# Dense attention: turning the probabilities by 32 by 32 squares and DMAs instead of on TensorE

## What is computed

```python
def _sparse_attention(x, src, dst, wq, bq, wk, bk, wv, bv, wo, bo):
    q = (x @ wq + bq).reshape(N, H, Dh) * Dh ** (-0.5)
    k = (x @ wk + bk).reshape(N, H, Dh)
    v = (x @ wv + bv).reshape(N, H, Dh)
    scores = jnp.einsum('ehd,ehd->eh', q[src], k[dst])
    smax = jax.ops.segment_max(scores, src, num_segments=N)
    ex = jnp.exp(scores - smax[src])
    denom = jax.ops.segment_sum(ex, src, num_segments=N)
    attn = ex / denom[src]
    out = jax.ops.segment_sum(attn[:, :, None] * v[dst], src, num_segments=N)
    return out.reshape(N, D) @ wo + bo

for i in range(4):
    y = _cond_layer_norm(x, cond, s1_w[i], s1_b[i], b1_w[i], b1_b[i])
    x = x + _sparse_attention(y, ...)
    y = _cond_layer_norm(x, cond, s2_w[i], s2_b[i], b2_w[i], b2_b[i])
    x = x + relu(y @ m_w1[i] + m_b1[i]) @ m_w2[i] + m_b2[i]
```

## Time and profile before

| | |
|---|---|
| median of 3 runs | 2674.96 us (2674.15 to 2680.72) |
| the profiled execution's own time | 2671.21 us |
| its span, first to last instruction | 2669.5 us |
| PE / DVE / ACT / POOL busy, share of the span | 97% / 52% / 32% / 15% |
| DMA traffic | 154.71 MB, mean 58 GB/s |

### The profile page before, as it was taken

The page is one execution under the profiler, slowest core; times in us unless marked ns, Lnnn a source line. Parts: engine busy times, 40 slices in busy tenths (PEclk is TensorE's granted clock), DMA queues, the critical chain, the costliest instruction groups (busy, mean ns, idle before and its releaser), DMA issues. The chain is left out here.

```text
span 2669.5 us, 29597 instructions
## 1 busy us (share of the span) xinstructions
PE 2578.7 (97%) x10736; PEld 1534.9 (57%) x10736; DVE 1396.1 (52%) x3067; ACT 850.7 (32%) x1775; POOL 397.7 (15%) x396
## 2 busy tenths in 40 slices
PE   8999899999999999999999999999999998999994
PEld 4665545456776555777555677655577754533341
DVE  7986741515665532666551566653266654523344
ACT  5875532212442120444111244312044412302221
POOL 2004120102000200200200200020020012515551
PEclk9999999999999999999999999999999999999997
DMA  6301011420000110000010000011000001569636
GB/s 172 121 21 48 1 43 45 114 67 24 1 1 1 41 36 23 18 1 1 22 39 32 24 1 1 1 41 36 18 22 1 1 17 55 189 198 328 215 89 212
DMA packets 84372, 154.71 MB, mean 58 GB/s; under 512 B 31909, under 2 KB 32389, under 8 KB 81887
## 3 DMA queue, kind: packets, MB, share of 16 engines
q1 hardware_dynamic: 60702, 106.12, 12.8%
q0 software_dynamic: 20784, 41.80, 4.8%
q10 hardware_dynamic: 2741, 4.89, 0.7%
HBM read 207.61 MB, written 27.34 MB: 88 GB/s over the span
## 5 line engine op out<-in xcount | busy, mean ns | idle before, releaser
L1942 ACT ACTIVATE g_prob<-g_prob,g_row_max 125x1250 f32<-125x1250 f32 x160 | 214.0, 1338 | 710.6 <-DVE g_row_max L1876 710.6
L1682 PE MATMUL psum<-cols,w 128*128 128x500 f32 (+1 forms) x1120 | 393.2, 510 | 1.2 <-PEq L88 1.2
L1744 PE MATMUL psum<-g_k_cols,g_q_cols 128*125 128x512 f32 (+1 forms) x960 | 362.9, 513 | 1.9 <-DVE g_row_max L1873 1.9
L1758 PE MATMUL psum<-cols,rows 125*128 125x250 f32 x1600 | 364.0, 374 | 0.1
L1758 PEld LDWEIGHTS psum<-cols,rows 125*128 125x128 f32 x1600 | 302.7, 189 | 34.6 <-issue 3.8
L1682 PEld LDWEIGHTS psum<-cols,w 128*128 128x128 f32 x1120 | 209.9, 189 | 173.1 <-issue 165.0
L1873 DVE CUSTOM_DVE_ANT_0 g_prob<-psum,ln_count 125x1250 f32<-125x1250 f32 x160 | 233.5, 1459 | 75.2 <-PE psum L1744 75.2
L1744 PEld LDWEIGHTS psum<-g_k_cols,g_q_cols 128*125 128x125 f32 x960 | 168.0, 187 | 161.8 <-issue 159.1
L1883 DVE COPY cols<-psum 125x500 f32<-125x500 f32 x160 | 108.6, 679 | 199.2 <-PE psum L1773 199.2
L1773 PEld LDWEIGHTS psum<-ident,g_prob 125*125 125x125 f32 x1600 | 199.4, 188 | 9.0 <-issue 1.9
L1996 POOL TENSOR_TENSOR xbuf<-xbuf,g_bias_rows 125x512 f32<-125x512 f32 x40 | 63.2, 1618 | 937.0 <-DVE rows L1617 937.0
(11 more groups left out here) (346 smaller groups left out, 3446.7 us busy)
## 6 DMA issues: line engine op xcount, KB each, us to landing
m_eb<-in_L_ffn_expert_b SPq DMA_DIRECT2D x54, 192.0 KB, 5.8
w<-in_L_gnn_m_w SPq DMA_DIRECT2D x8, 1024.0 KB
slot_rows<-p_kf SPq DMA_DIRECT2D x1, 7128.0 KB, 33.5
rows<-slot_rows SPq DMA_DIRECT2D x54, 132.0 KB, 3.4
m_ew<-in_L_ffn_expert_w SPq DMA_DIRECT2D x4, 1536.0 KB, 11.0
w<-in_L_mix_W SPq DMA_DIRECT2D x4, 1024.0 KB, 5.1
w<-in_L_gnn_wq SPq DMA_DIRECT2D x4, 1024.0 KB, 5.3
w<-in_L_gnn_wk SPq DMA_DIRECT2D x4, 1024.0 KB
```

Source lines behind the costliest of these rows:

```text
L1682: ins = c.pe.matmul(c.bank(group_bank(g), width), wt[:, k, o * 128:(o + 1) * 128], y_cols[:, k, start:start + width], start=(k == 0), stop ...
L1744: ins = pe.matmul(psum[0:P, start:start + width], q_cols[:, h, t * P:(t + 1) * P], k_cols[:, h, start:start + width], start=True, stop=True)
L1758: ins = pe.matmul(c.bank(6 + g % 2, 2 * P), v_rows[:, j, h * 128:(h + 1) * 128], turned_prob[:, g % 2, j, :], start=(j == 0), stop=(j == N ...
L1942: s.activation(prob[:, u, :], prob[:, u, :], ACT.Exp, bias=row_max[:, u, 1:2], accum_out=row_max[:, u, 2:3]).then_inc(exp_made, 1)
```

## The change

- The PE transposes (`turn_probs` on PE) and the copies of their results (on DVE and ACT) are gone. DVE instead turns the 128 x 1280 probabilities of a step in 32 x 32 squares in one instruction (`turn_squares`), from SBUF to a `square` buffer in SBUF. `prob` is widened to 128 x 1280 and cleared once by POOL.
- A square then still lies in the partition quarter of its queries. For each pair of steps SP issues 4 x 4 = 16 DMAs (`turn_sp`), one for each source and destination quarter, each of 32 partitions x 2560 contiguous bytes (80 KB), from `square` to `turned`, SBUF to SBUF. Each has two slots: `square` lies over w[0], w[1] and part of w[2], `turned` in the widened `cols`.
- The product with the reciprocal row sum goes from DVE to ACT (`normalise`).
- Scores alternate between banks 0 to 2 and 3 to 5, and `scores(n)` waits for the read of step n - 2 only.
- `weigh` runs five steps behind (WEIGH_LAG = 5, before 3). Keys are now in ten blocks of 128 (the last of 98), and a weighing matmul has 256 columns, in runs of 32, where it had 250 contiguous ones.
- At the end of the steps the order on PE is: rest of pair 17, outputs 0 and 1, pair 18, two norm starts, outputs 2, pair 19.
- wo has a buffer of its own, which it shares with the conditioning weights; these get their ones and zeros again in each layer. m_w1, m_w2 and the next wq are loaded only when the last DMAs of the turning have landed.

```diff
+SQUARE = 32
+KEY_BLOCKS = -(-N // 128)
+SIDE = 128 // SQUARE
+TURNED_SLOTS = 2
+TURNED_SLOT = 2 * KEY_BLOCKS * 128
...
+    WEIGH_LAG = 5
+    score_at = lambda n: n % 2 * 3 * BANK
...
+        wo = sb("g_wo", [128, KC, D])
+        cond_w = wo[0:COND_ROWS]
+        prob = sb("g_prob", [128, 2, KEY_BLOCKS * 128])
...
+        square = [w_flat[:, s * TURNED_SLOT:(s + 1) * TURNED_SLOT].rearrange("p (b u f) -> p b u f", b=SIDE, u=2)
+                  for s in range(TURNED_SLOTS)]
+        turned = [cols_mem[:, s * TURNED_SLOT:(s + 1) * TURNED_SLOT].rearrange("p (a u f) -> p a u f", a=SIDE, u=2)
+                  for s in range(TURNED_SLOTS)]
+        turned_keys = [turned[s].rearrange("p a u (j i) -> p j u a i", i=SQUARE) for s in range(TURNED_SLOTS)]
...
+        def turn_sp(l, g):
+            sp = c.sp
+            s, pair = g % 2, PAIRS * l + g
+            sp.wait_ge(squared, 2 * pair + 2)
+            if g >= 2:
+                sp.wait_ge(weighed, pair - 1)
+            for of in range(SIDE):
+                for to in range(SIDE):
+                    load(sp, turned[s][quarter(to), of], square[s][quarter(of), to]).then_inc(turned_in[s], 16)
...
+            for g in range(PAIRS):
+                if g == PAIRS // 2:
+                    sp.wait_ge(bo_added, NT * (l + 1))
+                    load_bias_row("m_b2", l)
+                turn_sp(l, g)
+            for s in range(TURNED_SLOTS):
+                sp.wait_ge(turned_in[s], 16 * SIDE * SIDE * PAIRS // 2 * (l + 1))
+            load_w(1, "m_w1", l)
+            load_w(2, "m_w2", l)
...
                 else:
-                    pe.wait_ge(score_read, STEPS * l + n)
+                    pe.wait_ge(score_read, STEPS * l + n - 1)
...
             def weigh(g, part):
                 h = 2 * g // NT
                 if part == 0:
-                    pe.wait_ge(turned_act, 2 * (STEPS * l + 2 * g + 2))
-                    pe.wait_ge(turned_dve, STEPS * l + 2 * g + 2)
+                    pe.wait_ge(turned_in[g % 2], 16 * SIDE * SIDE * ((PAIRS * l + g) // 2 + 1))
...
-            turn_probs(0)
             for n in range(2, STEPS):
                 scores(n)
-                if n >= 3:
-                    weigh((n - 3) // 2, (n - 3) % 2)
-                turn_probs(n - 1)
-            pe.wait_ge(w_in[0], 16 * (2 * l + 1))
+                if n >= WEIGH_LAG:
+                    weigh((n - WEIGH_LAG) // 2, (n - WEIGH_LAG) % 2)
+            weigh(PAIRS - 3, 1)
+            pe.wait_ge(wo_in, 16 * (l + 1))
             outputs(0)
+            outputs(1)
+            weigh(PAIRS - 2, 0)
             weigh(PAIRS - 2, 1)
-            turn_probs(STEPS - 1)
-            outputs(1)
+            norm_pe(2 * l, 0)
+            norm_pe(2 * l, 1)
+            outputs(2)
             weigh(PAIRS - 1, 0)
             weigh(PAIRS - 1, 1)
-            norm_pe(2 * l, 0)
-            norm_pe(2 * l, 1)
...
+            def turn_squares(n):
+                u, s, pair = n % 2, n // 2 % 2, PAIRS * l + n // 2
+                v.wait_ge(prob_made, STEPS * l + n + 1)
+                if n == 0:
+                    v.wait_ge(v_mm, NT * (l + 1))
+                if n % 2 == 0 and pair >= 2:
+                    v.wait_ge(turned_in[s], 16 * SIDE * SIDE * (pair // 2))
+                v.transpose(square[s][:, :, u, :].rearrange("p b (j i) -> p b j i", i=SQUARE), prob_squares[u]).then_inc(
+                    squared, 1)
...
-            turn_probs(0)
+            turn_squares(0)
+            invert_sum(1)
             for n in range(2, STEPS):
-                normalise(n - 1)
                 scores(n)
-                turn_probs(n - 1)
-            normalise(STEPS - 1)
+                turn_squares(n - 1)
+                invert_sum(n)
+            turn_squares(STEPS - 1)
...
+            for n in range(STEPS):
+                exp(n)
+                if n >= WEIGH_LAG + 1 and (n - WEIGH_LAG) % 2:
+                    take_out((n - WEIGH_LAG) // 2)
+                normalise(n)
```

More of the change, by code:

```diff
@@ L139, in build @@
             with c.stage():
[L140 removed]
+                gnn(c, x, ln_count, cond_parts, cond_w_parts, w_all, cols_mem, cols, rows, sum_dram)
         with c.stage():
@@ L1466, in performer, with gnn @@
         pool_end()
-def gnn(c, x, ln_count, cond_parts, cond_w_parts, w, y_cols, rows, sum_dram):
+def gnn(c, x, ln_count, cond_parts, cond_w_parts, w_all, cols_mem, y_cols, rows, sum_dram):
     nc, psum, ident, a = c.nc, c.psum, c.ident, c.a
+    w = [w_all[:, i] for i in range(3)]
     H = GNN_HEADS
@@ L1640, in layer_sp @@
             load_bias_row("bv", l)
[L1641 to L1646, removed]
+            if l >= 1:
+                sp.wait_ge(part_made, 3 * l)
+            load(sp, wo[:], weight_rows("L0_gnn_wo", l)).then_inc(wo_in, 16)
             sp.wait_ge(v_made, NT * (l + 1))
             load_bias_row("bo", l)
-            sp.wait_ge(bo_added, NT * (l + 1))
-            load_bias_row("m_b2", l)
+            sp.wait_ge(v_mm, NT * (l + 1))
+            for g in range(PAIRS):
[7 more added lines that the diff above has]
+            load_w(2, "m_w2", l)
             if last:
@@ L1655, in layer_sp @@
                 load(sp, v_rows, rows_view(sum_dram[:, :])).then_inc(sum_in, 16)
-                for n, done in enumerate(((o_mm, NT * L), (h_mm, 12 * L))):
-                    sp.wait_ge(*done)
+                for n in range(2):
+                    if n == 1:
+                        sp.wait_ge(h_mm, 12 * L)
                     load(sp, w[n][:].rearrange("p c o -> p (c o)")[:, 0:4 * FFN_I].rearrange("p (c o) -> p c o", c=2),
@@ L1757, in weigh @@
                 for j in range(5 * part, 5 * part + 5):
-                    ins = pe.matmul(c.bank(6 + g % 2, 2 * P), v_rows[:, j, h * 128:(h + 1) * 128],
-                                    turned_prob[:, g % 2, j, :], start=(j == 0), stop=(j == NT - 1))
+                    r = key_rows(j)
+                    ins = pe.matmul(c.bank(6 + g % 2, 256).rearrange("p (u a i) -> p u a i", u=2, a=SIDE),
+                                    rows[0:r, j, h * 128:(h + 1) * 128], turned_keys[g % 2][0:r, j],
+                                    start=(j == 0), stop=(j == KEY_BLOCKS - 1))
                 if part == 1:
                     ins.then_inc(weighed, 1)
[L1763 to L1775, removed]
             def outputs(t):
@@ L1783, in outputs @@
                 for k in range(KC):
-                    ins = pe.matmul(c.bank(t % 2, D, P), q_cols[:, k, t * P:(t + 1) * P], w[0][:, k, :],
+                    ins = pe.matmul(c.bank(t % 2, D, P), q_cols[:, k, t * P:(t + 1) * P], wo[:, k, :],
                                     start=(k == 0), stop=(k == KC - 1))
@@ L1941, in exp, with normalise @@
                 s.wait_ge(max_negated, STEPS * l + n + 1)
-                s.activation(prob[:, u, :], prob[:, u, :], ACT.Exp, bias=row_max[:, u, 1:2],
+                s.activation(prob[0:P, u, 0:N], prob[0:P, u, 0:N], ACT.Exp, bias=row_max[:, u, 1:2],
                              accum_out=row_max[:, u, 2:3]).then_inc(exp_made, 1)
+            def normalise(n):
+                u = n % 2
+                s.wait_ge(sum_step, 2 * (STEPS * l + n) + 2)
+                s.activation(prob[0:P, u, 0:N], prob[0:P, u, 0:N], ACT.Identity, scale=row_max[:, u, 3:4]).then_inc(
+                    prob_made, 1)
             def take_out(g):
@@ L1986, in layer_pool @@
             if l == 0:
-                for n, value in ((1, 0.0), (3, 0.0), (0, 1.0), (2, 1.0)):
-                    g.memset(cond_w[:, n, :], value).then_inc(ones_made, 1)
+                g.memset(prob[:], 0.0).then_inc(prob_blank, 1)
                 g.wait_ge(c.gnn_x_in, 16 * NT)
```

95 lines of the change are left out of this document (43 added, 52 removed).

## The result

The kernel after takes 2703.57 us (median of 4 runs, 2701.78 to 2705.65) beside 2674.56 for the kernel before (4 runs, 2673.25 to 2680.72): ratio 1.0108, 95% interval 1.0095 to 1.012. It is 29 us slower, where the forecast had 134 us slower.

A forecast was written before the change was run, and what follows sets the result against it. PE bound the kernel before; SP's queue would after, at 0.74 us a DMA. 18.2 + 319 x 0.74 + 3.4 + 4.34 + 4.1 = 266.1 us a layer against 232.6, +134 in all: 2809 us, range 2540 to 2870.

The forecast's parts named there:

- A step without SP: PE's time for one attention step after the change: 2.10 us of scores and 2.17 of weighing, 4.27 us together.
- The turning: DVE's turning instruction in each attention step, priced like the score pass at 1.50 us.
- Start to first issue: Start of a layer's steps: from the end of scores(0) until SP can begin its DMAs, 18.2 us.
- The gap behind pair 19: End of a layer's steps: with outputs(2) moved ahead, PE lies open waiting for the norm, 4.1 us a layer.
- the term 319 x 0.74: SP's queue over a layer's steps: from first to last of 320 DMA issues, at 0.74 us each.
- landing: End of a layer's steps: the last DMA lands 3.4 us after its issue.
- rival (B): Attention steps: no change in time, at an SP cadence of 0.635 us an issue; 2675 us, chance 0.07.
- The sign that the prediction set: Median issue of the new DMAs on SP: below 0.5 us it is (A), above 0.6 the forecast stands.
- (A): Attention steps: SP keeps up below 0.53 us an issue, PE sets the pace; -31.3 us a layer, 2550 us, chance 0.40.
- (C): DVE's turning takes 2.9 us; in (A) 28 us a layer come back, 2662 us; a tenth of (A)'s chance.
- (D): SP's queue in attention dearer, 0.79 us an issue: +49.4 us a layer, 2873 us; part of the forecast's side.
- PE's idle time also covers a spell of halved clock: Attention steps with SP as bound: PE's idle 3.3 us a pair absorbs halved-clock spells, priced at nothing.

The follow-up runs named there:

- the fillers: Unused matmuls on PE ahead of each pair's wait for its squares, added to the kernel after: 2699.40 us, ratio 1.0099.

## Why the prediction was wrong

**Right.** The bound moved to SP's queue, and the kernel got slower. A step without SP would be 4.27 us; measured 4.26. The turning: 1.50 taken, 1.506 measured. Start to first issue: 18.2 against 18.05. The bytes are hidden, as half of them showed. POOL's constants, wo, m_w1 and m_w2 cost nothing that PE's waits show. The gap behind pair 19: 4.1 forecast, 3.5 found (from the end of its matmuls, 1299.20 - 2.91 = 1296.29, to 1300.64, less the 0.86 that stood between outputs(2)'s end and outputs(3) before), and the two experiments on it show that moving outputs(2) back saves it only when PE is the bound.

**Wrong: the term 319 x 0.74.** The step that failed is "the nearest row by source and destination, by partitions and by size is the 0.74, and I take it". Measured over the layer: 0.655. That is 319 x 0.74 = 236.1 us against 208.8, 27.3 us a layer too much. The rest of the sum was off by little: landing 2.1 us (1289.6 to 1291.70) for 3.4, start -0.15, pair 19 +0.25, the gap -0.6. Together 27.3 + 1.3 + 0.15 - 0.25 + 0.6 = 29.1: 266.1 becomes 237.0, against 232.6 before, +4.4 in this layer instead of +33.5. The stretch to m_w1 has another 1.7 for outputs(3), which the sum did not have: +6.1.

The difference of two large terms, 43.6 us of transposes gone against SP's surplus, magnified an error of 13% in the cadence to a factor of over 4 in the result. That the measured time lies inside the range of 2540 to 2870 says little, since the range was made to span both ends. The kernel lies close to rival (B)'s point, 0.635; with 0.633 the sum gives 232.0, so that (B) was no thin case between two others but sat right where the third kind of row, the 64 partitions at 0.60, pointed. The sign that the prediction set, a median issue below 0.5 us for (A) and above 0.6 for the forecast, did not decide either: 0.591 lies between.

The prediction had the decisive doubt in writing, under (A): that 0.70 "may belong to 18 rows, a number that does not spread evenly". It argued it away with "all 24 SBUF to SBUF issues cost the same", but all 24 had 18 rows, and so could not tell the two explanations apart. The run with 18 rows did, at 2808 us. Its being within 1 us of 2809 is partly luck: the cadence of 0.74 is confirmed, but its four layers are 152 us longer than before the change, where the forecast had 134, and its expert stage is 13 us shorter. Why 18 rows cost the queue more stayed open.

**Rivals.** (A)'s total was right for the kernel with twelve DMAs, 2550 against 2551.37, in part by luck: -26.1 us a layer for its -31.3, and the expert stage made up most of the rest. Its condition for 16, a cadence below 0.53, was false. The estimate of 0.43 us an issue from 512 sequencer cycles that stood beside it ("DMA: Bandwidth & Descriptors" in the Trainium skill) is too low here: 0.59 on SP, 0.61 on ACT; and its word that the time to initiate a DMA is usually small beside the DMA does not carry over to many small ones from one queue, as four DMAs fewer a pair made 134 us in the layers. (C) is out at 1.506. (D), 0.79, is out.

**A price of 0 that was wrong in another way.** "PE's idle time also covers a spell of halved clock" holds inside the steps, as the fillers showed. It does not hold behind the last wait of a layer, where outputs(3) took 5.30 us for 3.60, 6.5 us in the four layers.

## What to carry to other kernels

Work taken off the bound engine and turned into many small DMAs is priced by the count of issues on one queue, here about 0.6 us each at 80 KB as at 40. Compare that count times the price with the time of a step before anything else. Four issues of sixteen, made into copies by an idle engine, decided between layers that are 107 us shorter in all and layers that are 30 us longer. When a price is borrowed from a row, ask in what ways all its cases are alike: if they all share one unusual number, the row can't say that the number doesn't matter. A time that comes out as forecast is checked term by term too: twice here other parts of the program made up a difference. Moves within the same partitions need no DMA, and an idle engine made them at 0.715 us a copy.

## What the runs showed that was not expected

- The price of an issue, SBUF to SBUF, on SP's queue: 32 partitions 0.591 us, 16 partitions 0.589, 18 partitions 0.698; bytes halved, 0.591. On ACT's queue 32 partitions took 0.613. 16 partitions from HBM had 0.31.
- DVE turns 128 x 1280 f32 in squares of 32 in 1.50 us, also beside POOL's copies of the same buffers.
- The expert stage, untouched by every edit, took 376 to 383 us in the kernels that leave out a part of the attention and 390 to 396 in the others. A kernel that leaves work out to test a theory can change a later stage whose work depends on the values, so a stage's own stretch has to be compared before an edit is given the credit.
